# Two-layer graph network on one core: row statistics of two tiles on ScalarE, its table at the head, one skipped branch as six

## The reference, cut to what matters

```python
h = relu(layernorm(x))                 # per row, over 512 features
# layer 0: batch norm of h, mean over in-edges, @ W_conv, relu;
#          plus linear attention over the nodes (8 heads, random features); plus h;
#          batch norm of the sum
x = x + layer0(h)
h = relu(layernorm(x))
# layer 1: (1 + eps) * h + segment_sum(h[src], dst); @ W1 + b1, batch norm, relu;
#          @ W2 + b2, batch norm, relu; plus h
x = x + layer1(h)
```

## Time and profile before

| | |
|---|---|
| median of 3 executions | 365.75 us (365.27 to 365.75) |
| the profiled execution's own time | 365.71 us |
| its span, first to last instruction | 363.9 us |
| TensorE busy | 349.3 us, 96% of the span |
| VectorE busy | 245.2 us, 67% |
| ScalarE busy | 181.7 us, 50% |
| GpSimd busy | 94.1 us, 26% |
| granted TensorE clock, mean | 0.997 |

### The profile page before, as it was taken

The page is one execution under the profiler, slowest core; times in us unless marked ns, Lnnn a source line. Parts: engine busy times, 40 slices in busy tenths (PEclk is TensorE's granted clock), DMA queues, the critical chain, the costliest instruction groups (busy, mean ns, idle before and its releaser), DMA issues.

```text
span 363.9 us, 6197 instructions
## 1 busy us (share of the span) xinstructions
PE 349.3 (96%) x2072; PEld 224.6 (62%) x2072; DVE 245.2 (67%) x666; ACT 181.7 (50%) x303; POOL 94.1 (26%) x163
## 2 busy tenths in 40 slices
PE   8999899989999999999998999999999999999994
PEld 4678655757777666767565675455555555565562
DVE  5889999998998995867996886522464453422325
ACT  0548538768477167454437766411533644233132
POOL 8132020000000000100042778722277465101100
PEclk9999999999999999999999999999999999999998
DMA  6990303300000000034900000000000000010223
GB/s 179 283 304 19 119 1 119 118 3 1 3 3 4 3 3 3 3 103 145 263 7 3 0 2 3 2 2 1 2 0 0 2 0 2 0 51 21 70 58 85
DMA packets 13539, 18.05 MB, mean 50 GB/s; under 512 B 1839, under 2 KB 6895, under 8 KB 13491
## 3 DMA queue, kind: packets, MB, share of 16 engines
q1 hardware_dynamic: 12538, 17.21, 16.3%
q10 hardware_dynamic: 953, 0.23, 0.3%
HBM read 14.88 MB, written 2.56 MB: 48 GB/s over the span
## 4 chain that ended last, share of the span: by engine, by line
PE 82%; DVE 6%; ACT 5%; issue 3%; POOL 2%; DMA 1%; DVEq 0%; SPq 0%; ACTq 0%; POOLq 0%
PE bank L1436 78%; PE bank L1466 2%; PE bank L1834 1%; POOL ln_s L491 1%; ACT hn L688 1%; PE bank L1793 1%; DVE st_row L1324 1%; ACT hh L832 1%; ACT sqr L694 1%; DMA edge<-src 1%; DVE x L1387 0%; PE bank L1647 0%; ACT hring L602 0%; DVE aggf L1344 0%; DVE hl L1305 0%
## 5 line engine op out<-in xcount | busy, mean ns | idle before, releaser
L1436 PE MATMUL bank<-AT,hh 125*128 125x400 f16 (+3 forms) x250 | 81.1, 332 | 1.0 <-DVE hl L1305 0.5
L1436 PE MATMUL bank<-AT,hl 125*128 125x400 f16 (+3 forms) x250 | 80.8, 331 | 0.0
L994 DVE TENSOR_SCALAR ring<-iota_code,code 125x250 f16<-125x250 f16 x200 | 46.1, 306 | 1.4 <-issue 1.4
L1436 PEld LDWEIGHTS bank<-AT,hh 125*128 125x128 f16 x250 | 24.1, 97 | 19.2 <-issue 1.1
L1436 PEld LDWEIGHTS bank<-AT,hl 125*128 125x128 f16 x250 | 24.2, 97 | 17.7 <-issue 0.2
L1436 PE MATMUL bank<-ring,S 125*128 125x250 f16 x200 | 33.5, 310 | 0.0
L1436 PE MATMUL bank<-a_hi,w_hi 128*128 128x400 f16 (+1 forms) x96 | 32.6, 339 | 0.0
L1436 PE MATMUL bank<-agg_hi,w_hi 128*128 128x400 f16 (+1 forms) x96 | 32.6, 339 | 0.0
L1436 PE MATMUL bank<-agg_hi,w_lo 128*128 128x400 f16 (+1 forms) x96 | 32.5, 338 | 0.0
L1436 PE MATMUL bank<-a_hi,w_lo 128*128 128x400 f16 (+1 forms) x96 | 32.5, 338 | 0.0
L1436 PE MATMUL bank<-agg_lo,w_hi 128*128 128x400 f16 (+1 forms) x96 | 32.5, 338 | 0.0
(11 more groups left out here) (236 smaller groups left out, 704.2 us busy)
## 6 DMA issues: line engine op xcount, KB each, us to landing
w_s<-w SPq DMA_DIRECT2D x4, 1024.0 KB, 5.0
x_in<-x SPq DMA_DIRECT2D x5, 448.0 KB
x<-x SPq DMA_DIRECT2D x2, 1120.0 KB
out<-x SPq DMA_DIRECT2D x6, 224.0 KB
wB<-wk SPq DMA_DIRECT2D x1, 1024.0 KB, 9.3
wA<-wq SPq DMA_DIRECT2D x1, 1024.0 KB, 14.3
wC<-w_conv SPq DMA_DIRECT2D x1, 1024.0 KB, 16.0
wB<-wv SPq DMA_DIRECT2D x1, 1024.0 KB, 6.0
```

The lines of the kernel that those rows point to most:

```text
L994: return dve.tensor_scalar(ring[:, slot, j, a:b], iota_code[0:CH, a:b], code[:, bass.ds(c + j, 1)], float(-CODES * t), ALU.subtract, ALU.i ...
L1436: return pe.matmul(o, l, r, start=start, stop=stop, skip_group_check=True)
```

## The change

Four edits:

- VectorE no longer makes the statistics of row tiles 8 and 9. ScalarE makes them in `row_squares`: one pass over the tile with a sum, the mean's negative from it, a second pass with the sum of squared differences. `hring` takes the values that nobody reads. The block of tile 8 stands behind rows 5, that of tile 9 behind rows 8 in the turn t = 1, and rows 9 moves to t = 2. GpSimd makes variance plus epsilon for the two tiles, with one instruction more each.
- ScalarE starts with a one-column Relu on `ones16`, which takes the table load with it. Its four DMAs are then issued when the edges have landed, and the wait for the constants comes behind them.
- The fillers at `ranges` are 3 and not 5.
- `agg1_extra` goes. Each of the six groups has its own branch over 20 products, ahead of its last two.

```diff
-SPARE = {"start": 20, "ranges": 5, "hT0": 3, "hT1": 3, "hT2": 4}
+SPARE = {"start": 20, "ranges": 3, "hT0": 3, "hT1": 3, "hT2": 4}
+SCALAR_STATS = (8, 9)
...
+        row_sums = place("row_sums", [L, 2, T], F32, 7.0625)
...
             for i in range(T):
-                pool.wait_ge(sem("s_mv"), i + 1)
+                if i < SCALAR_STATS[0]:
+                    pool.wait_ge(sem("s_mv"), i + 1)
+                else:
+                    pool.wait_ge(sem("s_squares"), i - SCALAR_STATS[0] + 1)
+                    own.step(pool.tensor_scalar(ln_tmp[:, 0, i:i + 1], row_sums[:, 1, i:i + 1], 1.0 / D, LN_EPS,
+                                                ALU.mult, ALU.add))
                 row_scales(i, 1, sem("s_rs"))
...
-            act.wait_ge(sem("s_const"), NCONST)
+            act.wait_ge(sem("s_ones"), 1)
+            act.activation(tables[:], ones16[:, 0:1], ACT.Relu).then_inc(sem("s_tables"), 1)
+            act.wait_ge(sem("d_edge"), 64)
             act.dma_start(par_r[:], params).then_inc(sem("d_par"), 16)
...
             act.dma_start(eps_col[:], eps.broadcast_to([P, 1])).then_inc(sem("d_par"), 16)
+            act.wait_ge(sem("s_const"), NCONST)
...
+            def row_squares(i):
+                n = 2 * (i - SCALAR_STATS[0])
+                act.wait_ge(sem(f"d_x{i // 2}"), 32)
+                act.activation(hring[:, i, :], x_tile(i), ACT.Copy, accum_out=row_sums[:, 0, i:i + 1])\
+                   .then_inc(sem("s_sums"), 1)
+                act.wait_ge(sem("s_sums"), n + 1)
+                act.activation(ln_tmp[:, 1, i:i + 1], row_sums[:, 0, i:i + 1], ACT.Copy, scale=-1.0 / D)\
+                   .then_inc(sem("s_sums"), 1)
+                act.wait_ge(sem("s_sums"), n + 2)
+                act.activation(hring[:, i, :], x_tile(i), ACT.Square, bias=ln_tmp[:, 1, i:i + 1],
+                               accum_out=row_sums[:, 1, i:i + 1]).then_inc(sem("s_squares"), 1)
...
             for i in range(4, 8):
                 rows(i)
+                if i == 5:
+                    row_squares(SCALAR_STATS[0])
...
                 if t == 1:
-                    for i in (8, 9):
-                        rows(i)
+                    rows(SCALAR_STATS[0])
+                    row_squares(SCALAR_STATS[1])
+                if t == 2:
+                    rows(SCALAR_STATS[1])
                 if t == SQ_AT:
                     conv_weights()
...
                 if t == 0:
-                    for i in range(6, T):
+                    for i in range(6, SCALAR_STATS[0]):
                         row_stats(i)
...
+                    if k == T - 1:
+                        with pe.If_lt(big_r, most_r):
+                            for j in range(T):
+                                for h in (hh, hl):
+                                    mm(ps[:, 0:w], h[:, j, fs], ATlo[:, j, c0:c0 + w], False, False)
+                        pe.end_ifs()
                     mm(ps[:, 0:w], hh[:, k, fs], AT[:, k, c0:c0 + w], k == 0, False)
                     ins = mm(ps[:, 0:w], hl[:, k, fs], AT[:, k, c0:c0 + w], False, k == T - 1)
                     if k == T - 1:
                         close_group(ins, name)
-
-            def agg1_extra():
-
-                pe.wait_ge(sem("s_hlb"), T)
-                with pe.If_lt(big_r, most_r):
-                    for f, ci in A1_FIRST:
...
                 turn_rows(i, hring1, 3, "s_hb", f"g{i}")
-                if i == T - 1:
-                    agg1_extra()
                 agg1_rows(i)
```

## The result

The changed kernel takes 367.74 us, the median of 12 executions (366.87 to 371.0); the kernel before takes 365.63 (365.27 to 365.84) in 12 executions on the same chip. The medians differ by 2.1 us: slower. The ratio, 1.0071 with a 95% interval of 1.0056 to 1.0086, is that of the means; the changed kernel's two slowest executions, 371.0 and 370.57, pull it above the 1.0058 of the medians. The forecast was 366.1 and no measurable change; the result lies 0.04 above the top of the range. What came is the rival of the falling clock, 0.4 dearer than its price of 367.3.

What follows compares the result with a forecast made beforehand. TensorE holds 82% of the chain, but from 44 to 79 us VectorE's time counts. From 365.71: head, relief, first block and branches 0, second block + 0.4, giving 366.1; own range 365.7 to 366.6, whole range 364.9 to 367.7.

Steps and rivals of the forecast that it cites:

- the rival of the falling clock: TensorE's granted clock falls in the gap before hT9, slowing hT9 and UK0: + 1.6 us, 367.3; chance 0.33.
- the forecast's own case: ScalarE's second block delays hT9 by 1.3 us, kmax and the end by 0.4: 366.1; chance 0.45.
- The rival's gap: TensorE stands from N0's end near 37.8 to hT9 at 40.96: about 3.1 us, twice the 1.53 before.
- ScalarE's load: Statistics blocks of 2.0 us each: tile 8's free before rows 6, tile 9's makes hT7's copy end at 40.82.
- the low row: Lower bound of one statistics block on ScalarE: passes of 0.59 us each, 1.78 in all; the high bound was 2.22.
- The table at the head: Earlier table load brings the first product with wk forward by 0.9 to 1.25 us; gone by hT5, counted as 0.
- VectorE's relief: Two statistics sets off VectorE give a 2.1 us lead, 0.9 usable before UK0, none if hT9 is late; counted 0.
- The rival's 364.8: If ScalarE's second block hid, hT9 stays at 39.65 and VectorE takes kmax 0.9 earlier: 364.8; chance 0.14.
- Rows 9: Moved behind Q1's copies but still in front of hT7's copy on ScalarE, so it changes nothing there.
- The branches: Six short branches near 226 us cost 0, as VectorE sets the next groups at 229.22; at worst a 1.7 loss.

Runs made afterwards that it cites:

- the first experiment: The changed kernel with 12 filler products on TensorE between N0 and hT9 (also called the filled kernel): 366.37 us, ratio 1.0023 to the kernel before.
- three kernels (364.75, 364.79, 364.9): The changed kernel with W_conv's sum of squares at t = 3; that with the parameter DMAs back; the latter with only tile 8 on ScalarE, rows 9 at t = 1.

## Why the prediction was wrong

**The step that failed** is the last of the forecast's own case: that TensorE's longer gap costs only its length, so that kmax is 0.4 late. In its place the granted clock fell in the gap, and kmax was 1.84 late, 1.38 of it by the slower hT9 and UK0. The mechanism in front of it was right, though its number was hit by luck, as the next part but one shows. hT7's copy was forecast for 40.82 and ended at 40.83; hT9 was forecast for 40.96 and came at 40.97. With the clock held (the first experiment) kmax came at 42.70, forecast 42.66, and the median was 366.37, forecast 366.1. But the text itself said that the gap would be twice as long as one during which the clock held, and that at the kernel's end the clock had fallen 1.7 us behind the last transpose. It gave that row less weight because the work before it was thin. It was the only row with a stop longer than those of up to 1.58 in which the clock held, and it pointed the right way, so the clock rival deserved more than its 0.33. But that it said 1.7 was luck too. At the end of the changed kernel the last transposes are over at 361.84 and the clock falls near 365.1, 3.2 us later (busy time by stretch, kernel after):

```profile
364.50:365.00 0.50, 0.00 (x0) 0.00 (x0) 0.00 (x0) 0.00 (x0) 0.00 (x0) 1.00 0.87 239
365.00:365.50 0.50, 0.00 (x0) 0.00 (x0) 0.00 (x0) 0.00 (x0) 0.00 (x0) 0.57 0.07 21
```

Over the twelve profiled executions of the kernels here, the fall at the end comes in nine 1.7 to 3.7 us after the last product, in one at 4.05, and in two, which end 4.0 and 4.1 after it, not at all. One row of this kind can't price a rival.

The rival's gap was wrong as well. N0 was over at 38.12 before, so it couldn't be over at 37.8 when it comes later; it ended at 38.43, behind the transposes of hT7 and hT8, and the gap was 2.54, not 3.1.

**The clock rival was under-priced by 0.4.** It allowed 1.2 for the fall of at most 1.67; the runs show 1.37. It allowed 0.4 for the late hT9; the filled kernel shows 0.7, with kmax 0.46 late. About 0.15 more is an idle time of 0.33 before VectorE's `S` at 55.75 in the filled kernel. It stands in the profiled executions of the four kernels that have both tiles on ScalarE and in no other; the profile names no releaser, and its cause is open. (With one tile moved instead of two, TensorE's last stretch starts at 87.11 instead of 87.49 in the profiled executions; the medians, 364.9 and 364.79, don't show it.) The rest is within what medians of these kernels move by. Nor is it shown that such a delay of kmax always reaches the end in full: with the statistics back on VectorE kmax stood at 42.68 in the profiled execution, as late as in the filled kernel, and that execution took 365.78 and not 366.28.

**Three errors in ScalarE's load cancelled**: -0.24 for the block, +0.45 in front of it, -0.2 for the overlap of the copies. That hT7's copy came within 0.01 of its forecast is luck. The block takes 1.76, not 2.0: the passes start 0.53 and 0.63 before the accumulator reads behind them, nearer to the Square's 0.59 than to the 0.81, so the low row was the one to take. The 0.45 of GpSimd's power and shift wasn't foreseen at all; it is also why hT5 came at 30.52 and not near 30.0. With tile 8 alone moved, where that power takes 0.55, it came at 30.09. Removing work from VectorE moved an operation forward into one that ScalarE waits for. The statistics' place was costed, not what takes it.

**The table at the head** was rightly counted at nothing, with a wrong number on the way: 0.9 to 1.25 forecast at the first product, 0.17 in the profiled execution, since wk landed 1.0 later than before. That number varies: in the other kernels with early DMAs the product stands between 14.07 and 15.11. The text named the packets in front of wk and gave them too little. With the DMAs back that product stands at 14.08, 14.11 and 14.35, inside or just above the 13.9 to 14.3 forecast.

**VectorE's relief** was taken as a lead of 2.1 of which 0.9 could be used before UK0. The kernels with `sqr` later used 1.05, and it wasn't UK0 that ate the rest but the wait at 37.17. The rival's 364.8 was met by three kernels (364.75, 364.79, 364.9), none of them the change as made.

**Rows 9** were said to change nothing by moving behind Q1's copies. In the changed kernel that holds, since ScalarE has no idle time there. With tile 8 alone the same move costs 1.9.

**The branches** cost nothing, as forecast: no gap between the pairs, and VectorE sets the next groups. The first product follows VectorE's last hl after 0.30 in the changed kernel, before after 0.42; the gain is hidden behind VectorE.

## What to carry to other kernels

When a change lengthens a gap on TensorE, price the gap as its length plus the slower work behind it, and look in the trace for the gap that is nearest in length, wherever it is, and in more than one execution: here the slower work cost 1.37 and the rest 0.7. When work is taken off an engine, ask what moves into the freed place and which engine it then runs beside. And before an engine is relieved, move what stands in front of the next copy: one constant made this change from 2.1 us slower into 0.9 us faster, where alone it was worth nothing.

## What the runs showed of the hardware

- **The clock in TensorE's gaps.** The granted clock stayed at 1.00 in the gaps of 1.52 and 1.53 before hT9 in the five profiled executions that have one, and in that of 1.65 near 80 in the changed kernel. In the profiled execution with a gap of 2.54 it fell near 40.8, some 2.4 us after the last product, and was back near 44.2; in the one with 2.22 it fell near 40.6, some 2.6 after the last product, when work had returned. By the mean clocks it fell in most executions of that kernel. Of the changed kernel's 12 executions only the fastest, 366.87, reaches the range of the kernel with the gap filled. Fillers in the gap kept it at 1.00. At the end of the kernels, with nothing behind, it fell from 1.7 us after the last product on, in two of twelve executions not within 4.0. The Trainium skill (TensorE: Matmul & The Clock Gate, Part 1) has the gate's free-running phase as the reason why the same kernel's transition comes at different points from run to run. That two of the twelve executions with the gap of 2.22 kept a mean of 1.00 and ten didn't fits that, and no run here tests it.
- **Executions with far lower clocks.** The slowest of the changed kernel (371.0 and 370.57, mean clock 0.977) lost more than one such gap explains. Where else the clock was down in them isn't known, as they weren't the profiled ones.
- **GpSimd's power on one column** takes 0.55 or 0.56 in most places, 0.93 beside VectorE's `S`, in both kernels, and 0.61 to 0.81 where VectorE makes `ring` meanwhile.
- **Small DMAs ahead of a large one.** With four parameter DMAs issued some 1.7 us earlier from another queue, the 1 MB of wk landed 9.1 to 10.4 us after its issue in six profiled executions; without, 7.9 to 9.3 in six others. The means are 1.2 apart, and the two ranges overlap.
- **A tile of x that lands late** makes VectorE's third statistics wait 0.30, 0.34 or 1.03 in three of the twelve profiled executions and not in the others, with the DMAs early or not. What makes it late isn't shown.
